# Relational graph layer on one core: rows loaded ahead of x, narrower comparisons, and every 72nd chunk fetched row by row by SyncE

## What is computed

```
seg  = dst * R + edge_type
sums = segment_sum(x[src], seg, N * R).reshape(N, R, F)
cnt  = segment_sum(1, seg, N * R).reshape(N, R, 1)
conv = einsum('nri,rio->no', sums / max(cnt, 1), W_rel) + x @ W_root + bias
h    = conv + x @ W_res + b_res
h    = relu((h - mean(h)) * rsqrt(var(h) + 1e-5) * gamma + beta)
out  = layernorm(x + h)
```

## Time and profile before

| | us |
|---|---|
| median of 3 runs | 2063.9 (2062.92 to 2065.56) |
| the profiled execution | 2066.09 |
| its span in the trace | 2063.3 |

### The profile page before, as it was taken

The page is one execution under the profiler, slowest core; times in us unless marked ns, Lnnn a source line. Parts: engine busy times, 40 slices in busy tenths (PEclk is TensorE's granted clock), DMA queues, the critical chain, the costliest instruction groups (busy, mean ns, idle before and its releaser), DMA issues.

```text
span 2063.3 us, 38048 instructions
## 1 busy us (share of the span) xinstructions
PE 1928.5 (93%) x13298; PEld 1799.5 (87%) x13298; DVE 1379.7 (67%) x2530; ACT 1482.5 (72%) x1650; POOL 1513.0 (73%) x1581
## 2 busy tenths in 40 slices
PE   5899999999999999999999999999999999999997
PEld 3899888899889888888889888888988988988987
DVE  6877676676666666666667667667666666666656
ACT  5878767677767767777777776776776776777763
POOL 6777777777777777777777777777777777777760
PEclk9999999999999999999999999999999999999999
DMA  8744544444544544444444454454454444444443
GB/s 290 202 102 107 111 102 106 112 101 107 112 103 107 112 100 106 106 112 102 106 112 104 107 112 100 107 112 101 107 113 103 106 107 102 106 106 102 105 109 107
DMA packets 244737, 233.85 MB, mean 113 GB/s; under 512 B 27097, under 2 KB 239491, under 8 KB 243907
## 3 DMA queue, kind: packets, MB, share of 16 engines
q0 software_dynamic: 223056, 203.79, 44.4%
q1 hardware_dynamic: 21491, 27.60, 4.3%
HBM read 218.48 MB, written 12.80 MB: 112 GB/s over the span
## 4 chain that ended last, share of the span: by engine, by line
PE 66%; DMA 20%; POOL 7%; issue 4%; ACT 1%; DVE 1%; SPq 0%; ACTq 0%; POOLq 0%; DVEq 0%
PE tb L642 30%; PE ps L612 23%; DMA xg<-xtab,srcT 20%; PE ps L618 8%; POOL xg L507 6%; PE tb L542 4%; ACT agg L745 1%; POOL wsb L498 1%; DMA wsb<-in_x_dram,srcT 0%; DVE lst L1169 0%; DVE agg L1193 0%; DMA eth<-in_edge_type_dram 0%; PE ps L719 0%; PE ps L730 0%; PE ps L731 0%
## 5 line engine op out<-in xcount | busy, mean ns | idle before, releaser
L507 POOL DMA_INDIRECT xg<-xtab,srcT x1545 | 1486.6, 962 | 473.1 <-issue 247.4
L745 ACT ACTIVATE agg<-ps 128x390 f32 (+1 forms) x1563 | 1439.8, 925 | 521.8 <-PE ps L618 410.1
L980 DVE TENSOR_SCALAR onehot<-iota,segT,vT 128x456 fp32r<-128x456 f32 x1563 | 1120.5, 742 | 393.7 <-PE ps L618 385.2
L642 PE MATMUL tb<-agg,wsb 128*128 128x144 f32 x6370 | 1134.2, 304 | 4.9 <-ACT agg L745 3.5
L612 PE MATMUL ps<-onehot,xg 128*128 128x390 f32 (+1 forms) x3126 | 977.4, 395 | 93.0 <-DMA xg<-xtab,srcT 88.3
L642 PEld LDWEIGHTS tb<-agg,wsb 128*128 128x128 f32 x6370 | 869.2, 191 | 5.2 <-ACT agg L745 3.7
L612 PEld LDWEIGHTS ps<-onehot,xg 128*128 128x128 f32 x3126 | 489.2, 190 | 179.3 <-DMA xg<-xtab,srcT 140.3
L618 PEld LDWEIGHTS ps<-onehot,xg 128*128 128x128 f32 x2930 | 541.0, 189 | 3.8
L618 PE MATMUL ps<-onehot,xg 128*128 128x66 f32 x2930 | 448.7, 234 | 0.0
L998 DVE SCALAR_TENSOR_TENSOR tmph<-iota,lastg,tb 128x72 f32<-128x72 f32 x98 | 27.8, 284 | 144.3 <-PE tb L642 142.1
L542 PE MATMUL tb<-same,identb 128*128 128x512 bf16 x416 | 108.1, 384 | 3.3 <-DVE same L920 3.3
(11 more groups left out here) (129 smaller groups left out, 330.6 us busy)
## 6 DMA issues: line engine op xcount, KB each, us to landing
xg<-xtab,srcT POOLq DMA_INDIRECT x1545, 2.8
xtab<-agg SPq DMA_DIRECT2D x4, 1536.0 KB
hinit<-H SPq DMA_DIRECT2D x1, 3125.0 KB, 10.7
agg<-in_x_dram SPq DMA_DIRECT2D x4, 768.0 KB, 7.2
out_dram<-agg SPq DMA_DIRECT2D x6, 448.0 KB, 3.0
dsth<-in_dst_dram SPq DMA_DIRECT2D x23, 64.0 KB
eth<-in_edge_type_dram SPq DMA_DIRECT2D x23, 64.0 KB
srcr<-in_src_dram SPq DMA_DIRECT2D x12, 64.0 KB
```

The lines of the kernel that those rows point to most:

```text
L507: pool.indirect_dma_start(out=xg[c % RING][:], out_offset=None, in_=xtab.bitcast(F32R), in_offset=bass.IndirectOffsetOnAxis(ap=srcT[t % 2] ...
L642: ins = nc.tensor.matmul(o, wsb[:, r * F:(r + 1) * F], pair_rhs(p, r), start=(r == 0), stop=(r == R - 1))
L745: nc.scalar.activation(agg_group(g)[:, bass.ds(off, n), :], ps[c % NPS][:, 0:n * R].rearrange("f (n r) -> f n r", r=R), ACT.Copy).then_inc ...
L980: nc.vector.tensor_scalar(onehot[o][:].rearrange("p (a b) -> p a b", a=3), iota3[:, :, 0:IW], segT[t % 2][:, k:k + 1], vT[t % 2][:, k:k + ...
```

## The change

There are three parts.

**Start.** The rows of tile 0 are loaded by six DMAs instead of eight: one DMA now brings whole rows of 256 entries (1 KB) of `dsth`, and one of `eth`, with their halos. SP waits for them before it issues the loads of x. The weights and the four columns are issued by ACT, behind the same wait. The pieces of the table lie elsewhere in `agg`, so that ACT waits for three pieces ahead of `evacuate(0)` and for the rest ahead of chunk 32. POOL still waits for all of them. ACT's first table load is caused by a tiny copy that waits for nothing but `consts`.

**Comparisons.** Comparison j of a tile leaves out the first 56 - 8j columns: 136 of 192 for j = 0, 192 for j = 7.

**Chunks by SP.** Chunks 110, 182, ... 1550 (21 of them) are no longer gathered by POOL. SP loads the chunk's 128 source numbers into one partition, reads them into registers four at a time, and issues one DMA of 1 KB for each row, into `xf` (two buffers). ACT rounds `xf` to fp32r in `xs` with one instruction of 128x256, six chunks ahead of its use. POOL's ring goes by its own count.

```
+SP_FIRST = 110
+SP_EVERY = 72
+SP_LOAD = 182
+NSX = 2
+XS_AHEAD = 6
...
+    by_sp = list(range(SP_FIRST, NCH - 1, SP_EVERY))
+    by_pool = [c for c in range(NCH) if c not in by_sp]
...
+                def spans(vec, lo, m):
+                    return bass.AP(tensor=vec.tensor, offset=vec.offset + lo, ap=[[P, m], [1, HW]])
...
-                            sp.dma_start(tile[0:1, HALO:P], vec[0:HALO].rearrange("(a e) -> a e", a=1)).then_inc(rows_in, 16)
-                            sp.dma_start(tile[1:TC, 0:P], rows(vec, HALO, n - HALO)).then_inc(rows_in, 16)
+                            sp.dma_start(tile[0:1, HALO:HW], vec[0:HW - HALO].rearrange("(a e) -> a e", a=1)).then_inc(rows_in, 16)
+                            sp.dma_start(tile[1:TC, :], spans(vec, P - HALO, TC - 1)).then_inc(rows_in, 16)
                         else:
-                            sp.dma_start(tile[:, 0:P], rows(vec, a - HALO, a - HALO + n)).then_inc(rows_in, 16)
-                        sp.dma_start(tile[:, P:HW], rows(vec, a + HALO, a + HALO + n)).then_inc(rows_in, 16)
+                            sp.dma_start(tile[:], spans(vec, a - HALO, TC)).then_inc(rows_in, 16)
...
             sp.wait_ge(cleared, 3)
             load_rows(0)
+            sp.wait_ge(rows_in, 16 * row_loads(0))
             for q in range(4):
...
+            def gather_rows(n):
+                s = n % NSX
+                if n >= NSX:
+                    sp.wait_ge(xs_rdy, n - NSX + 1)
+                sp.wait_ge(snum_in[n % 2], 16 * (n // 2 + 1))
+                for q in range(0, P, 4):
+                    nodes = nc.values_load_multi_w_load_instructions(
+                        snum[n % 2][0:1, q:q + 4], engines=[ENG.SP], min_val=0, max_val=N - 1,
+                        skip_runtime_bounds_check_because=NODES)[1]
+                    for i in range(4):
+                        sp.dma_start(xf[s][q + i:q + i + 1, :], xtab[bass.ds(nodes[i], 1), :]
+                                     ).then_inc(sgath[s], 16)
...
+            for n in range(RING, len(by_pool)):
+                c = by_pool[n]
...
-                pool.wait_ge(agg_ps, c - RING + 2)
+                pool.wait_ge(agg_ps, by_pool[n - RING] + 2)
...
+            def round_rows(n):
+                act.wait_ge(sgath[n % NSX], 16 * P * (n // NSX + 1))
+                if n >= 1:
+                    act.wait_ge(agg_ps, by_sp[n - 1] + 2)
+                nc.scalar.activation(xs[:], xf[n % NSX][:], ACT.Copy).then_inc(xs_rdy, 1)
...
-            act.wait_ge(tab_out, 16 * 5)
+            act.wait_ge(tab_out, 16 * 3)
...
                 evacuate(c, offs[c % 4])
+                if c + XS_AHEAD in by_sp:
+                    round_rows(turn_of[c + XS_AHEAD])
...
                 h, n = j % 2, SB // 2
+                lo = HALO - (j + 1) * n
...
-                nc.vector.tensor_tensor(o, here, shifted(j * n + 1, n), ALU.is_equal).then_inc(cmp_rdy, 1)
+                nc.vector.tensor_tensor(o, here, shifted(lo + j * n + 1, n, EW - lo), ALU.is_equal).then_inc(cmp_rdy, 1)
```

More of the change, by code:

```diff
@@ L44 @@
 EPS = 1e-5
+NODES = "the sources are numbers of nodes"
 CLAMPED = "the offsets are clamped to the aggregation region when they are made"
@@ L100, in last_of_group @@
         return c % GC == GC - 1 or c == NCH - 1
+    by_sp = list(range(SP_FIRST, NCH - 1, SP_EVERY))
+    assert all(c % TC for c in by_sp) and SP_FIRST >= RING
+    by_pool = [c for c in range(NCH) if c not in by_sp]
+    turn_of = {c: n for n, c in enumerate(by_pool)} | {c: n for n, c in enumerate(by_sp)}
     def pair_len(p):
@@ L121, in gnn @@
         xg = [sb(f"xg{s}", [P, 2 * F], F32R) for s in range(RING)]
+        xf = [sb(f"xf{s}", [P, 2 * F], F32) for s in range(NSX)]
+        xs = sb("xs", [P, 2 * F], F32R)
+        snum = [sb(f"snum{s}", [1, P], I32) for s in range(2)]
         onehot = [sb(f"onehot{s}", [P, OW], F32R) for s in range(NOH)]
@@ L173, in gnn @@
         XST = (XT + 1) * 2 * F
[L174 to L178, removed]
+        XS0 = PREG - 3 * XPIECE * 2 * F
+        XN0 = XS0 + XST
+        XN1 = XN0 + (XT + 1) * F
+        assert XS0 >= 512 and XN0 >= PREG and XN1 + 512 <= 2 * PREG
+        pieces = agg[:, XS0:XN0].rearrange("p (t f) -> p t f", f=2 * F)
+        stage = agg[:, XS0:XN0].bitcast(F32R).rearrange("p (t f) -> p t f", f=2 * F)
+        xnat = agg[:, XN0:XN1].rearrange("p (t f) -> p t f", f=F)
+        rest = agg[:, XN1:2 * PREG]
+        head = agg[:, 0:XS0]
         WLO = R - RING
         first_x = wsb[:, WLO * F:R * F].rearrange("p (c f) -> p c f", f=F)
-        xTs = [xT, rest[:, 0:512], rest[:, 512:1024]]
+        xTs = [xT, rest[:, 0:512], head[:, 0:512]]
         xin = agg[:, PREG:PREG + NT * P].rearrange("p (t f) -> p t f", f=F)
@@ L237, in gnn @@
         tab_out = sem("tab_out")
+        tab_rest = sem("tab_rest")
         srcf_rdy = sem("srcf_rdy")
@@ L255, in gnn @@
         gath = [sem(f"gath{s}") for s in range(RING)]
+        sgath = [sem(f"sgath{s}") for s in range(NSX)]
+        snum_in = [sem(f"snum_in{s}") for s in range(2)]
+        xs_rdy = sem("xs_rdy")
         agg_ps = sem("agg_ps")
@@ L306, in gnn, with root_x @@
         block = ctx.enter_context(nc.Block())
+        def root_x(b):
+            return xTs[b % NXT if b < UP else b % 2]
         def root_bank(b):
@@ L408, in _, with numbers @@
                          w_rel[0:WLO].rearrange("r p f -> p r f")).then_inc(w_in, 16)
[L410 to L419, removed]
+            def numbers(n):
+                c = by_sp[n]
+                sp.dma_start(snum[n % 2][:], src[c * P:(c + 1) * P].rearrange("(a e) -> a e", a=1)
+                             ).then_inc(snum_in[n % 2], 16)
@@ new lines, in _ @@
+            sp.wait_ge(raw_free, 1)
+            load_rows(1)
+            sp.wait_ge(first_lo, RING)
+            sp.dma_start(wsb[:, WLO * F:R * F].rearrange("p (r f) -> p r f", f=F),
+                         w_rel[WLO:R].rearrange("r p f -> p r f")).then_inc(w_in, 16)
+            numbers(0)
+            sp.wait_ge(up_h, UP)
+            sp.wait_ge(root_h, NROOT - UP)
+            sp.dma_start(hinit, H[:, 0:N]).then_inc(hinit_out, 16)
+            sp.wait_ge(tab_out, 16 * 3)
+            sp.wait_ge(tab_rest, 16 * 2)
@@ L421, in fast @@
+            loaded = 1
+            for n, c in enumerate(by_sp):
+                if loaded + 1 < NTL and c >= (loaded - 1) * TC + SP_LOAD:
+                    loaded += 1
+                    sp.wait_ge(raw_free, loaded)
+                    load_rows(loaded)
+                if n + 1 < len(by_sp):
+                    numbers(n + 1)
+                gather_rows(n)
+            assert loaded == NTL - 1
             def fast():
@@ L610, in aggregate @@
                 for part in range(2):
-                    rows = xg[s][:, part * F:(part + 1) * F]
+                    rows = rows_in_sbuf(c)[:, part * F:(part + 1) * F]
                     ins = nc.tensor.matmul(ps[c % NPS][:, 0:w], rows, onehot[o][:, 0:w], start=(part == 0),
```

64 lines of the change are left out of this document (38 added, 26 removed).

## The result

The changed kernel takes **2034.41 us** (median of 4 runs, 2032.43 to 2035.39) against 2064.73 us (2062.92 to 2067.21) for the kernel before on the same chip. The ratio is **0.9851**, 95% interval 0.9838 to 0.9864. The forecast was 2035, with a range of 2022 to 2062. The profiled execution has a span of 2032.4 us, 30.9 less than before, at a granted clock of 0.99.

What follows compares the result with a forecast made beforehand. POOL's stream of gathers was taken as the bound. Terms -26.1 (chunks), -6.3 (comparisons) and +3 (start) sum to -29.4 us from the profiled 2066.09, giving 2036.7; with the median 2.2 lower, 2035, range 2022 to 2062.

Steps and rivals of the forecast that it cites:

- POOL's stream is the path: Whole run: POOL's gathers, first to last, set the time at 1.24 us each; PE is faster and waits for POOL.
- rival C: Mid-run: a new wait, PE near the comparisons or ACT's late rounding, loses 13 to 15 us, 2048 to 2060; 8%.
- -26.1 for the chunks: POOL's gather stream: 21 gathers leave it at 1.244 us each, saving 26.1 us, with nothing in their place.
- SP keeps up at 0.58 us a row: SP's row fetches: 0.50 to 0.58 us a row, 64 to 74 us a chunk, against 89.5 us available; cost nothing.
- rival A: SP's row fetches: SP is the bound at 0.75 us a row, 96 us a chunk, giving 2168 us; 17%.
- Comparisons -6.3: DVE's narrower comparisons hold POOL's gathers for less time: 6.3 us saved, bounds 0 and -11.
- the even phase: Gathers against comparisons: a gather's start falls evenly over its 1.244 us pitch; average hold 0.27 us, then 0.20.
- Rival B: Comparisons hold POOL as before, by the skill page's rule or an unlucky phase: -23 us, 2041; 15%.
- Start +3: Before chunk 20's gather: rows landing later delay it from 47.33 to 50 to 51 us; +3 us, bounds -3 and +7.
- Chunk 11 lands later by 3 to 4: Start: chunk 11 of x lands 3 to 4 us later, delaying the chain that POOL's chunk 20 waits for.
- so the table follows at +4: Start: the table lands 4 us later, by 46 to 47 instead of 42.2 us.
- Rival D: Start worse than +7: table waits for x, x for rows, weights for ACT; 10 to 15 us, 2042 to 2047; 5%.

Runs made afterwards that it cites:

- split rows: Changed kernel with tile 0's 127-row loads split into DMAs of 112 and 15 rows: 2024.57 us, 0.9796 of the kernel before; other chip 2419.55 us, 1.0043.
- the first kernel that ran there: Kernel before with the narrower comparisons alone, on the chip where PE is the bound: 2407.43 us, 0.9994 of the kernel before.
- the two kernels that differ by it alone: Kernel before with narrower comparisons alone, 2052.88 us, and the same plus chunks by SP, with the kernel before's start, 2030.96 us.
- every-56th kernel: Changed kernel with every 56th chunk fetched by SP instead of every 72nd (26 chunks): 2149.16 us, 1.0413 of the kernel before.
- changed, second profile: Changed kernel run again unaltered: 2034.01 us, 0.9853 of the kernel before.
- x at once (other chip): Changed kernel without SP's wait for the rows ahead of x, on the chip where PE is the bound: 2430.26 us, 1.0089 of the kernel before.
- the old start: Changed kernel with the kernel before's row loads, table place and order of x, weights and rows: 2030.96 us, 0.9823; other chip 2422.81 us, 1.0059.
- every 60th chunk: Changed kernel with tile 0's rows on 16 and 15 DMA engines and every 60th chunk by SP (25 chunks): 2020.22 us, 0.9786 of the kernel before.

## Why the prediction was right

**POOL's stream is the path: right.** The split rows moved its beginning by 10 and its end by 12 us, and the run by 11.5 by the ratios; the narrower comparisons took 13.9 off the gathers and 13.9 off the run. On the other chip the comparisons brought nothing, and the page of the first kernel that ran there says why: PE's idle time is ended by "issue" and ACT instead of by a gather. In mid-run no gather of the changed kernel waits for a buffer and no rounding for its rows, so that rival C is out too.

**-26.1 for the chunks: right as 21 pitches,** but more than the runs show for the part by itself. Between the two kernels that differ by it alone the last gather moved by 21.3 and the median by 21.9, since the gathers that were left took 4.8 us more. 3.5 us of that are plain gathers that took slightly longer. Whether SP's row fetches cause it, or it is the spread between runs, isn't settled.

**SP keeps up at 0.58 us a row: right,** 74.65 and 74.6 us a chunk against 74. It was put together from three rows of other kinds. The parts held as well: 0.25 us for a one-row DMA, measured 0.225; 0.18 for the address from a register, measured 0.18; 0.10 for the register load, measured 0.15. The threshold stood at 89.5 us; rival A's 96 us came from the 0.43 us of a 128-partition load, which a one-row DMA doesn't cost. The every-56th kernel shows that A's mechanism is real and its price as steep as was feared: 5.4 us too few for each chunk turned -1.5% into +4.1%.

**Comparisons -6.3: mechanism right, size off.** Measured -11.2 between the two traces, just beyond the bound of -11. (The formula's own terms give -6.6.) Its totals were near: 28.7 us against 26 predicted before, 17.1 against 19.5 after. What failed is the even phase. Before, it gives 96 x 0.83 / 1.244 = 64 gathers of 0.41 us; 54 were held, by 0.53 us each. After, it gives 96 x 0.71 / 1.244 = 55; 48 were held, by 0.36 us each, and 40 to 49 in the other kernels with the same widths and 16-bit numbers on chips like this. The starts are far from even: 28 of the 96 comparisons of the changed kernel start with 1.1 to 1.2 us left to the next gather, where an even phase gives 8, and in eight of the twelve tiles exactly four of the eight comparisons catch a gather. A likely reason, not shown, is that a comparison is queued between two `onehot` instructions and so keeps a place relative to POOL's pitch. Rival B is out. The Trainium skill's statement quoted in the prediction ("SBUF — State Buffer", section "Who interferes with whom"), by which the two shouldn't meet and which the page itself calls inferred, is not what any run here shows: every kernel's trace has held gathers, 33 to 94 of them.

**Start +3: too small, +5.1.** The rows landed 4.9 us later, forecast 4.4, at 43 ns a packet, forecast 42. Two terms behind that were too small. These are the times that bear on them, in us:

| kernel | POOL's first gather | table's last write issued | `onehot(0)` | `evacuate(0)` | chunk 20's gather |
|---|---|---|---|---|---|
| before | 14.70 | 29.15 | 35.34 | 42.37 | 47.33 |
| changed | 19.60 | 37.95 | 44.99 | 47.82 | 52.47 |
| changed, second profile | 19.17 | 37.15 | 44.17 | 46.22 | 51.92 |
| x at once (other chip) | 20.59 | 34.32 | 40.48 | 48.71 | 53.50 |
| rows split | 9.81 | 27.60 | 34.61 | 37.66 | 42.51 |

"Chunk 11 lands later by 3 to 4" was one: `evacuate(0)`, which waits for its rounding, came 5.5 us later, and chunk 20's gather follows it by 4.7 to 5.0 us in the first two rows and in the fourth. So the chain that the prediction names, from chunk 11's landing through `evacuate(0)` and `root_product(6)`, is the right one, and it begins with the rows. The other was "so the table follows at +4". x was issued at 15.83 instead of 7.57, 8.3 us later, and the last write of the table went out 8.8 us later. DVE subtracts the pieces among its comparisons of tile 0, and it also waited 1.48 us for the last column, which ACT now loads behind the rows; before it did not wait there. So `onehot(0)` was 9.7 us late, and POOL's chunk 18 stood until 49.38 for PE; in the second profile (the run beside every 56th) it stood until 49.42 for the table. Two pitches on, that alone puts chunk 20 at 51.9. The two limits are within a microsecond of each other in the changed kernel. The kernel with x at once has the table and `onehot(0)` some 4 us earlier and gains nothing; with the rows split both come early, and the table is the last. Rival D's loads behind the rows are there, then, but they are not 10 us. Compared as runs, the old start is worth 0.9853 - 0.9823 = 0.0030, 6 us, though the two intervals leave room for 2 to 10.

**The sum.** -29.4 was forecast for a span that changed by -30.9 and a median that changed by -30.3. That it fits so well is in part luck: the errors of comparisons (-5) and start (+2) point opposite ways, and the tail's +1.2 was not in it.

## What to carry to other kernels

When one engine issues work at a fixed pitch and never waits, price a change by its instructions and by the time they are held, and check the start and the tail: what moved the stream's first gathers here moved its end. A start can have two chains that end within a microsecond of each other; then shortening one of them brings nothing. Check too that the engine is the path on the chip at hand; where another engine is slower, the same edit can cost. An idle queue can take over a share of the work up to a sharp threshold, its time per piece against the time between pieces: beyond it every piece adds its deficit. Here every 60th chunk still fitted and every 56th did not.

Count a load's engines before moving anything behind it. The 127 rows here set one DMA engine to work alone, and waiting for it cost more than the reordering brought.

## What the runs showed of the hardware that was not expected

- A gather's issue on POOL is held by a DVE tensor_tensor (a comparison, 16-bit or 32-bit operands) only if it starts within it. A held gather ends 0.81 us after the comparison (0.809 to 0.815 for nine in ten of 663 in all traces). One that starts 0.11 us ahead isn't held at all. The boundary is unsharp by some 0.03 us: 11 gathers that start 0.002 to 0.016 us after a comparison weren't held in the trace of the kernel before, and on the chip of the first four experiments some that start up to 0.034 us ahead were.
- A DMA of one row of 1 KB whose address comes from a register takes SP 0.225 us to issue, and with register loads and gaps 0.583 a row, at a steady pace over 3328 rows.
- Two chips differ by 17% on this kernel (2409 against 2065 us) with the same gathers. PE's granted clock is 0.92 against 0.99, and it pauses by about 1 us between matmuls where the profile shows nothing to wait for. The cause isn't known. What was 1.5% faster on the one was not tried unaltered on the other; its nearest relatives were 0.4 to 0.9% slower there.
